# A three-block decoder layer in one kernel: first-stage work moved from DVE to ACT and POOL, FFN activations transposed by DMA, loops written out

## What is computed

```python
x = x + attn(layernorm(x))      # qkva = rmsnorm(x)*gamma @ w_qkva; kv scanned over time with gate a; q * kv
x = x + xattn(layernorm(x), ctx)# 16 heads, 64 context keys + 1 null key; out projection, layernorm, scale and bias
x = x + ffn(layernorm(x))
# ffn: every product is quantized
_weight_quant(w): scale = 1/clip(mean|w|,1e-5);        clip(round(w*scale), -1, 1)/scale
_act_quant(x):    scale = 127/clip(max|x|,1e-5);       clip(round(x*scale), -128, 127)/scale
gate = silu(bitlinear(x, w_gate)); up = bitlinear(x, w_up)      # 256 -> 1024
return bitlinear(gate * up, w_down)                              # 1024 -> 256
```

## Time and profile before

| quantity | value |
|---|---|
| runs | 567.63, 564.99, 566.80 us; median 566.8 us |
| span of the profiled execution, first to last instruction | 562.9 us |
| busy: PE, DVE, ACT, POOL | 512.4, 479.9, 349.1, 301.1 us |
| mean granted TensorE clock | 0.989 |
| stage 1 / fold / stages 2 and 3 | to about 115 / 115 to 176 / 176 to 563 us |

### The profile page before, as it was taken

One profiled execution on the slowest core, in us unless ns is written; L12 is line 12 of the kernel. 1 busy time (PEld: TensorE's weight loads), 2 busy tenths in 40 slices (PEclk: granted clock), 3 DMA queues, 4 the chain that ended last, 5 costly groups with the idle time before them and its releaser, 6 DMA issues. The chain is left out here.

```text
span 562.9 us, 11113 instructions
## 1 busy us (share of the span) xinstructions
PE 512.4 (91%) x3226; PEld 419.2 (74%) x3226; DVE 479.9 (85%) x1017; ACT 349.1 (62%) x476; POOL 301.1 (53%) x451
## 2 busy tenths in 40 slices
PE   2889999998998888999999999999999999998765
PEld 1667778765787787888788888888887888885533
DVE  5899998969535767799999999999999999997884
ACT  4422341432142323578988888889889888885764
POOL 3112216500000467787777867776878677777740
PEclk9999999999999999899999999999999999999988
DMA  8991000000000000000000000000000000000001
GB/s 283 369 394 39 1 1 0 1 1 1 0 1 0 1 2 2 0 2 20 11 10 12 19 9 9 10 18 9 9 19 9 9 9 19 9 10 15 15 19 38
DMA packets 14925, 19.80 MB, mean 35 GB/s; under 512 B 1328, under 2 KB 12848, under 8 KB 14896
## 3 DMA queue, kind: packets, MB, share of 16 engines
q1 hardware_dynamic: 14896, 19.44, 9.9%
HBM read 15.24 MB, written 4.19 MB: 35 GB/s over the span
## 5 line engine op out<-in xcount | busy, mean ns | idle before, releaser
L495 POOL TENSOR_TENSOR region_d<-region_d,rden 128x1024 f32<-128x1024 f32 x32 | 60.9, 1902 | 124.5 <-DVE rden L990 124.5
L1120 PE MATMUL psum<-Mhi,xT2hi 128*128 (+1 forms) x256 | 74.8, 292 | 1.9 <-DVE xT2lo L947 1.6
L1120 PE MATMUL psum<-Mlo,xT2hi 128*128 (+1 forms) x256 | 72.4, 283 | 0.0
L1120 PE MATMUL psum<-Mhi,xT2lo 128*128 (+1 forms) x256 | 72.3, 283 | 0.0
L1373 PE MATMUL psum<-VW,region_d 128*128 (+1 forms) x256 | 61.9, 385 | 6.3 <-DVE pTn L1031 6.3
L1392 PE MATMUL psum<-VW,region_d 128*128 (+1 forms) x256 | 62.9, 389 | 0.0
L1373 PEld LDWEIGHTS psum<-VW,region_d 128*128 128x128 f32 x256 | 48.4, 191 | 16.2 <-DVE pTn L1031 7.6
L973 DVE TENSOR_REDUCE mx<-psum 128x8 f32<-128x520 f32 x64 | 44.6, 697 | 8.0 <-PE psum L1120 5.9
L1392 PEld LDWEIGHTS psum<-VW,region_d 128*128 128x128 f32 x256 | 47.1, 193 | 5.4
L1120 PEld LDWEIGHTS psum<-Mhi,xT2hi 128*128 128x128 f32 x256 | 48.2, 188 | 3.0 <-issue 2.7
L1120 PEld LDWEIGHTS psum<-Mlo,xT2hi 128*128 128x128 f32 x256 | 48.3, 189 | 0.0
(11 more groups left out here) (153 smaller groups left out, 1403.3 us busy)
## 6 DMA issues: line engine op xcount, KB each, us to landing
out_dram<-xs SPq DMA_DIRECT2D x32, 128.0 KB, 1.7
xs<-in_x_dram SPq DMA_DIRECT2D x1, 2560.0 KB, 16.4
VW<-in_L_xattn_Wkv_dram SPq DMA_DIRECT2D x1, 2048.0 KB, 17.2
region_b<-in_L_xattn_Wkv_dram SPq DMA_DIRECT2D x1, 2048.0 KB, 17.1
xs<-in_x_dram SPq DMA_DIRECT2D x3, 512.0 KB, 6.5
region_w<-in_L_ffn_w_gate_dram SPq DMA_DIRECT2D x1, 1024.0 KB, 10.1
region_w<-in_L_ffn_w_up_dram SPq DMA_DIRECT2D x1, 1024.0 KB, 12.5
region_w<-in_L_ffn_w_down_dram SPq DMA_DIRECT2D x1, 1024.0 KB, 16.8
```

The source lines that it names most:

```text
L495: pool.tensor_tensor(p2[:, v, 0:H * MK].rearrange("p (h j) -> p h j", j=MK), e[:, :, 0:MK], rden[:, v, :].unsqueeze(2).broadcast_to([P, H, ...
L1120: mm = pe.matmul(dst, lhsT, rhs, start=i == 0, stop=i == len(terms) - 1)
```

## The change

In stage 1, ACT now copies the transposed y from PSUM to SBUF (into `yTs`, which uses the place of `bd`) and POOL adds it to `xs`; DVE's statistics of the new `xs` come one step later. POOL also makes the inputs of the powers. ACT sums the absolute weights (Abs with accumulation). POOL clamps the rounded weights, and the rounding and clamping are spread over steps 3 to 7. After stage 1, ACT instead of DVE copies the transposed up weights (`wuT`).

In stages 2 and 3, ACT copies both halves of the probabilities. ACT writes the scaled hidden layer as int16 (`nq3`), and POOL casts it to bf16 (`nh3`), in place of DVE's subtraction. SP issues a transposing DMA for it and one for the FFN input; PE's transpositions and ACT's copies of both are gone. The down product and the residual of a tile come one step later. All loops are written out.

```diff
-        S1 = (-2, 2, NG - 2, NG + 1, 2)
-        S23 = (-2, 8, T - 4, T + 6, 4)
+        def groups(step):
+            for g in range(-2, NG + 1):
+                step(g, g % 2)
+        def steps(step):
+            for n in range(-2, T + 7):
+                step(n, n % 4)
# SP
-            with sp.Fori(0, T) as t:
-                sp.wait_ge(x3_done, t + 1)
-                sp.dma_start(out_t[:, t, :], xs[:, t, :]).then_inc(stored, 16)
+            def stages2_3(n, u4):
+                u, v = u4 % 2, 1 - u4 % 2
+                if exists(n - 6, T):
+                    sp.wait_ge(nh_ready, n - 5)
+                    if positive(n - 7):
+                        sp.wait_ge(down_psum, n - 7)
+                    sp.dma_start_transpose(nhT3[u], nh3).then_inc(nhT_ready[u], 16)
+                if exists(n - 3, T):
+                    sp.wait_ge(n3_ready, n - 2)
+                    if positive(n - 4):
+                        sp.wait_ge(up_psum, n - 4)
+                    sp.dma_start_transpose(nT3[:, v, :, :], n3[:, v, :]).then_inc(nT_ready[v], 16)
+                if exists(n - 7, T):
+                    sp.wait_ge(x3_done, n - 6)
+                    sp.dma_start(out_t[:, n - 7, :], xs[:, n - 7, :]).then_inc(stored, 16)
# POOL, stage 1
+                    pool.tensor_scalar(pw_in[:, 0:GT], mv1[:, :, 1], 1.0, 1e-5, ALU.mult, ALU.add)
+                    pool.tensor_scalar(pw_in[:, GT:2 * GT], mv1[:, :, 1], 0.0, None, ALU.max)
                     pool.tensor_tensor(pw_out[:, :], pw_in[:, :], expo[:, :], ALU.pow).then_inc(pw_done, 1)
                 if exists(g - 1, NG):
+                    pool.wait_ge(yT_copied, g)
+                    pool.tensor_tensor(rows, rows, yTs, ALU.add).then_inc(x1_done, 1)
+                if exists(g - 2, NG):
+                    deviation2(g - 2)
+                # g == 3: scaled(0), rounded(0); 4: ternary(0), scaled(1); 5: rounded(1), ternary(1)
+                # 6: scaled(2), rounded(2); 7: ternary(2)
...
+                pool.tensor_scalar(tern[i], raw[i], 1.0, -1.0, ALU.min, ALU.max).then_inc(tern_ready, 1)
# POOL, stages 2 and 3
+                    pool.wait_ge(hq_done, n - 5)
+                    pool.tensor_copy(nh3, nq3).then_inc(nh_ready, 1)
...
-                    pool.tensor_scalar(n3[:, v, :], z3[:, v, :], MAGIC, QMAX, ALU.subtract, ALU.min) \
+                    pool.tensor_scalar(n3[:, v, :], z3[:, v, :], 1.0, -MAGIC, ALU.mult, ALU.add) \
# ACT
+                    act.activation(yTs, banks(6, 2).rearrange("p b (t d) -> p (b t) d", d=D), ACT.Copy)
...
+                act.activation(tern[i], raw[i], ACT.Abs, accum_out=absum[:, i:i + 1])
...
+                    act.wait_ge(pT1_psum, n + 1)
+                    act.activation(pT[:, HC // 2:HC, :], bank(5).rearrange("p (c n) -> p c n", n=P), ACT.Copy)
...
-                    act.activation(hidden(n - 6), hidden(n - 6), ACT.Identity, bias=MAGIC, scale=qr[:, u, 0:1])
+                    act.activation(nq3, hidden(n - 6), ACT.Copy, scale=qr[:, u, 0:1])
...
-                    act.activation(nhT3.rearrange("p k n -> p (k n)"), bank(4).bitcast(BF16), ACT.Copy)
# DVE
-                    dve.tensor_tensor(rows, rows, banks(6, 2).rearrange("p b (t d) -> p (b t) d", d=D), ALU.add)
-                    dve.tensor_copy(pT[:, HC // 2:HC, :], bank(5).rearrange("p (c n) -> p c n", n=P))
-                    dve.tensor_scalar(nh3, hidden(n - 6), MAGIC, QMAX, ALU.subtract, ALU.min)
# PE
-                    for k in range(FC):
-                        mm = pe.transpose(bank(4).bitcast(BF16)[:, k * P:(k + 1) * P], nh3[:, k * P:(k + 1) * P],
-                                          ident16[:, :])
-                group(bank(5, D), [(nhT3[:, k, :], wdT[:, k, :]) for k in range(FC)])     # tile n-6
+                group(bank(5, D), [(nhT3[v][:, k, :], wdT[:, k, :]) for k in range(FC)])  # tile n-7
```

More of the change, by code:

```diff
@@ L322, in decoder_layer @@
         n3_ready = sem("n3_ready")
-        nT_psum = sem("nT_psum")
-        nT_ready = sem("nT_ready")
+        nT_ready = [sem(f"nT_ready{i}") for i in range(2)]
         gate_psum = sem("gate_psum")
@@ L331, in decoder_layer @@
         nh_ready = sem("nh_ready")
-        nhT_psum = sem("nhT_psum")
-        nhT_ready = sem("nhT_ready")
+        nhT_ready = [sem(f"nhT_ready{i}") for i in range(2)]
         down_psum = sem("down_psum")
@@ L445, in _, with scaled @@
             pool.memset(ones[:, :], 1.0).then_inc(consts_set, 1)
[L446 removed]
             pool.wait_ge(consts_set, 2)
[L449 removed]
+            def scaled(i):
                 pool.wait_ge(wrecip_done, 1)
@@ L463, in stage1 @@
                 if exists(g - 1, NG):
-                    pool.wait_ge(ve2_done, g)
-                    pool.tensor_tensor(rstd2[:, bass.ds((g - 1) * GT, GT)], ve2[:, :], expo[:, 0:GT], ALU.pow) \
-                        .then_inc(rstd2_done, 1)
-                if isinstance(g, int) and g == NG - 2:
+                    rows = xs[:, (g - 1) * GT:g * GT, :]
+                    pool.wait_ge(yT_copied, g)
+                    pool.tensor_tensor(rows, rows, yTs, ALU.add).then_inc(x1_done, 1)
+                if exists(g - 2, NG):
+                    deviation2(g - 2)
+                if g == 3:
+                    scaled(0)
                     rounded(0)
+                if g == 4:
+                    ternary(0)
+                    scaled(1)
+                if g == 5:
                     rounded(1)
-                if isinstance(g, int) and g == NG - 1:
+                    ternary(1)
+                if g == 6:
+                    scaled(2)
                     rounded(2)
-            tiles(pool, stage1, *S1)
+                if g == 7:
+                    ternary(2)
+            groups(stage1)
+            pool.wait_ge(x1_done, NG)
+            pool.memset(f["bd"], 0.0).then_inc(bd_zero, 1)
             pool.wait_ge(q_psum, NG)
             pool.memset(nvsel, 0.0).then_inc(nvsel_zero, 1)
+            deviation2(NG - 1)
             pool.wait_ge(ln_loaded, 32)
@@ L586, in _ @@
                 act.activation(w1hi[:, k, :], w1[:, k, :], ACT.Copy, scale=gcol[:, k:k + 1]).then_inc(w1_hi, 1)
-            tiles(act, stage1, *S1)
+            groups(stage1)
             act.preload_act_table(ACT.Exp)
@@ L885, in stage1 @@
                     dve.reciprocal(wrecip[:, :], wscale[:, :]).then_inc(wrecip_done, 1)
-            tiles(dve, stage1, *S1)
+            groups(stage1)
             def null_key(k):
@@ L1105, in stages2_3 @@
                 if exists(n - 5, T):
-                    dve.tensor_scalar(hw[:, v:v + 1], qs[:, v, 0:1], wscale[:, 2:3], None, ALU.mult) \
+                    dve.tensor_scalar(hw[:, (n - 5) % 4:(n - 5) % 4 + 1], qs[:, v, 0:1], wscale[:, 2:3], None, ALU.mult) \
                         .then_inc(hw_done, 1)
-                if exists(n - 6, T) and not (isinstance(n, int) and T - 1 <= n < T + 5):
-                    residual(n - 6, u)
-            tiles(dve, stages2_3, *S23)
+                if exists(n - 7, T) and not late(n):
+                    residual(n - 7)
+            steps(stages2_3)
         @block.tensor
@@ L1185, in stage1 @@
                     mm.then_inc(ctxT_psum, 1)
-                if isinstance(g, int) and g == 1:
+                if g == 2:
                     pe.wait_ge(absum_done, 3)
-                    pe.wait_ge(x1_done, 1)
+                    pe.wait_ge(yT_copied, 2)
                     group(bank(6, 3), [(ones[:, :], absum[:, :])]).then_inc(tot_psum, 1)
-            tiles(pe, stage1, *S1)
+            groups(stage1)
             def weight_T(i):
@@ L1399, in stages2_3 @@
                     gate_up(n + 1, u)
-                if exists(n - 6, T):
-                    pe.wait_ge(nhT_ready, n - 5)
+                if exists(n - 7, T):
+                    pe.wait_ge(nhT_ready[v], 16 * ((n - 7) // 2 + 1))
                     pe.wait_ge(pT1_ready, upto(n + 1, T))
-                    if positive(n - 6):
-                        pe.wait_ge(x3_done, n - 6)
-                    group(bank(5, D), [(nhT3[:, k, :], wdT[:, k, :]) for k in range(FC)]) \
+                    if positive(n - 7):
+                        pe.wait_ge(x3_done, n - 7)
+                    group(bank(5, D), [(nhT3[v][:, k, :], wdT[:, k, :]) for k in range(FC)]) \
                         .then_inc(down_psum, 1)
-            tiles(pe, stages2_3, *S23)
+            steps(stages2_3)
 _INS = ['x', 'ctx_2048', 'L0_attn_w_qkva', 'L0_attn_gamma', 'L0_xattn_Wq', 'L0_xattn_Wkv', 'L0_xattn_null_kv',
```

211 lines of the change are left out of this document (90 added, 121 removed).

## The result

The changed kernel takes 581.8 us (median of 4 runs, 580.1 to 582.4), the one before 565.9 in the same session (4 runs, 564.9 to 567.6): ratio 1.027, 95% interval 1.024 to 1.030. It is 15.9 us slower, where 0.8 us less was forecast. Its profiled execution spans 580.2 us, 17.3 more than the 562.9 of before.

The account below looks back on a forecast made before the run. Taken as bound: in stages 2 and 3 a chain through DVE, POOL and ACT, with PE and DVE nearly full. Stage 1 +1.7, first tiles -2.8, pairs -0.6, end +0.9 gave -0.8, so 566.0 us; range 552 to 596.

Parts of the forecast that it names:

- the part on the end: Last steps: -1.0 for steps without scores and contention, +1.9 for the last tile's down product, together +0.9 us.
- L: Time of the hidden layer's transposing DMA (256 KB): taken as 4.1 us, between 1.7 and 6.5; exposed only for the last tile.
- slow cast: Rival, stages 2 and 3: POOL's cast takes 3.6 us, each pair 2.4 longer, +29, about 595 us; chance 0.13.
- The chain: Stages 2 and 3: DVE, POOL, ACT to Silu decides the pair of tiles; 22.15 us becomes 22.1, -0.6 over about 12 pairs.
- C: Length of POOL's new cast of 128x1024 in stages 2 and 3, between probabilities and scalars: taken as 1.12 us.
- The first tiles: Tiles before any FFN work: DVE's copy L1036 leaves their shorter chain in about four tiles, -2.8 us.
- The hold: Stage 1: DVE's L811, with two SBUF inputs, waits for POOL's add, +1.9 us a group; y1 every 11.5 us.
- The sums: Stage 1: absolute weight sums move from DVE to ACT; 2.8 us count in step 0, 2.2 for the third: -5.0.
- The clamps: Stage 1: POOL's weight clamp of 2048 columns, bounded by 1.95 and 7.0 us, taken as 7.0, costing +4.3.
- No hold: Rival, stage 1: POOL's add does not stop L811, five groups gain 1.5 each, -7.5, so 558.6 us; chance 0.12.
- PE as the bound: Rival, stages 2 and 3: PE sets the pace, a pair falls to 20.8 us, -16, about 550 us; chance 0.10.
- The queue of transposing DMAs: Rival: ten blocks per tile in series take 17 us a tile, +155 over 26 tiles, about 720 us; chance 0.07.

Follow-up runs that it names:

- a: Changed kernel with, in the last steps, DVE's residual of tile n-7 moved to the end of the step: 562.4 us, 0.992 of the kernel before.
- b: Changed kernel with, in the last steps, PE's down product put ahead of gate and up of the next tile: 561.5 us, 0.990 of the kernel before.
- l: Kernel before, with DVE's residual in the last steps that of tile n-6 in place of n-7: 589.4 us, 1.039 of the kernel before.
- d: Changed kernel with the FFN input of the last four tiles transposed by PE and copied by ACT, not by DMA: 575.6 us, 1.016 of the kernel before.
- k: Run i with the hidden layers of the last two tiles transposed by PE and copied by ACT, not by DMA: 549.4 us, 0.969 of the kernel before.
- j: Kernel before, with only the copy of the second half of the probabilities moved from DVE to ACT: 569.9 us, 1.006 of the kernel before.
- e: Kernel before, with all of the change's stage 1 and stages 2 and 3 as before: 566.9 us, 1.001 of the kernel before.
- g: Changed kernel with the moves of both a and b: 560.2 us, 0.989 of the kernel before.
- f: Run b with POOL's stage 1 addition of y moved behind DVE's scale: 557.6 us, 0.984 of the kernel before.
- h: Run g with f's move of POOL's addition: 556.7 us, 0.983 of the kernel before.
- i: Run h with ACT's sum of the third weight one step earlier in stage 1: 552.1 us, 0.975 of the kernel before.

## Why the prediction was wrong, step by step

**The step that failed** is in the part on the end: "In the other steps the transposed data is needed more than a step (11 us) after it is made, which hides L." That holds in the body. In the last steps it fails twice. The input is needed at once there, because PE's next gate waits for it; and the down product came a step later while DVE's residual of these steps did not, so that the residual fell into the loop. In the code down went from n-6 to n-7, and `residual(n - 7, v)` of the last steps became `residual(n - 7)`, the same tile as before; I costed the shift at nothing without asking what reads the product. I also wrote of "two steps without scores", and seven more with FFN work alone follow them. The term was +0.9 and measured +24.3. Of this about 20 is the loop (a: -19.4, b: -20.3, l: +22.6 in the other direction), of which the landing itself is about 5 (d), and the last tiles are 2.3; some 2 us are left that no run takes apart. The time lies inside my 552 to 596, but by luck: the upper part of that range stood for a slow cast, which did not come.

**The last tile.** L was taken as 4.1 and is 3.06 for 256 KB; +1.9 was forecast. The stretch from the last hidden product to the end is 11.9 before and 14.3 after, +2.3: the shorter landing is made up by the cast's wait for its buffer (1.0) and by the lower clock (the down product takes 1.89, not 1.05). k confirms the place.

**The body.** The chain was right, its size too small. DVE's part fell by 1.7 (1.35 forecast, and the wait of 0.27 for PE went too), POOL's rose by 1.0 (forecast 1.2 with the hand-over), ACT's by 0.2 (0.57, less the slack behind Silu). A pair is 0.53 shorter, not 0.05 (my own 20.95 + 1.12 gives 0.08), and the body 5.3 us, not 0.6. C is 1.04, or 1.12 from start to next start, as taken. DVE waits 1.0 to 1.8 us for Silu in the steps shown, as the chain theory says; PE idles 1.5 us in 50, less than the 1.2 a pair that I gave. One branch was missing from the chain, the one over ACT's scaled layer and DVE's rounding: j shows that it had no room for the copy, and here it did no harm only because the rounding left DVE too.

**The first tiles.** -2.8 forecast, -3.4 measured between tiles 0 and 8. Of the 1.7 lost ahead of tile 0, 1.5 is the clock in this one execution: its matmuls there take 0.42 in place of 0.28 us (granted clock 0.83 from 185 to 195; 1.00 in a, b, e and g). That the 1.7 equals the +1.7 forecast for stage 1 is luck. Profiled executions of the same code up to there differ as much: tile 0 is at 194.62 in a and at 192.88 in b.

**Stage 1.** The hold was right in place and size: +1.9 and a wait of 0.6 forecast, 2.2 and 0.8 measured, y1 every 11.8 and not 11.5. The Trainium skill, "GPSIMD Engine Reference", section 8 (Key points), says that GpSimd shares its SBUF interfaces with VectorE and contends with instructions in a two-port mode or of two SBUF inputs. Runs e and f agree for the second kind: beside POOL's add only operations with two SBUF inputs were held, until the add ended. The sums gave 2.9 at the start, as forecast (2.8); the five groups behind it cost +3.2, where 4.0 less 2.2 for the third sum was forecast, clamps aside. The clamps were mis-sized: 1.89, the lower bound, not 7.0, and cost nothing (+4.3 forecast). And -1.6 for the transition did not come: PE is busy 19.6 of 20 us in the last groups, and DVE then waits 6.8 us for it. In sum +0.1 at the first probabilities (184.25 against 184.12), +1.7 forecast.

**The rivals.** No hold: refuted, and taking the hold out is worth 3.5 us by h, 8 together with i's edit. PE as the bound: not borne out in the body, where DVE waits for Silu, and where in the kernel before a copy moved to ACT alone lengthened the pair (j); no run took load off PE alone. Slow cast: refuted (1.04 us). The queue of transposing DMAs: it keeps up, and PE waits for no transposition between 260 and 500. The Trainium skill, "VectorE: DVE Perf Modes", section "The three transpose paths", gives 1309 ns for a block of 128x128; eight blocks land here in 3.1 us and two in 2.3, so blocks do not go one after the other at that price, and the estimate of 620 us was far off. The Trainium skill, the same page, section "Rules for kernel authors", advises TensorE for a 128x128 transposition where PSUM will do; that holds in the last steps (d, k), where latency counts, and for the body no run of the changed kernel tried it. None of my rivals had the loop. The slower side got 0.36, for the wrong reasons.

## What to carry to other kernels

When a producer in a software pipeline moves by one step, look at every consumer in the prologue and the epilogue, which are written apart: one that keeps its place can turn a loop over two steps into a loop over one, and there every latency counts in full. Price the steady state and the drain separately; in the drain little work of other tiles is left to hide a landing, and PE, mostly idle here, ran at a mean clock of 0.62. And before an operation is moved from one engine to another, walk each input of the next join: its other branch may have no slack, as in j.
